# Both layer norms' normalised tiles made on GpSimd instead of ScalarE

## The chip, the cores and the metric

The kernel runs on one core of one Trainium2 chip. Its time is the device time of one execution in microseconds (us). The engines are TensorE (PE in the profile, with PEld for its weight loads), VectorE (DVE), ScalarE (ACT), GpSimd (POOL) and SyncE (SP), which issues most of the DMAs. Each engine runs its own list of instructions in order; they meet through semaphores.

## The reference

The kernel computes one transformer block over x of shape (8, 512, 128), that is 8 batches of 512 tokens with 128 channels. Only what matters here:

```python
def _layernorm(x, axis=-1, eps=1e-05):
    m = jnp.mean(x, axis=axis, keepdims=True)
    v = jnp.var(x, axis=axis, keepdims=True)
    return (x - m) / jnp.sqrt(v + eps)

x = x + attention(_layernorm(x))     # 16 heads of 8 channels, rotary, causal softmax, W_proj
x = x + experts(_layernorm(x))       # gate logits, 8 Sinkhorn rounds, top-64 tokens for each of 8 experts
```

The gate logits and the expert products read the second norm; q, k and v read the first.

## The kernel before, in words

A batch's 512 tokens lie as 4 tiles of 128 tokens by 128 channels (`X[:, TB * b + t, :]`, `TB` = 4). VectorE takes each tile's mean and variance (`statistics`, `statistics2`), into `MV` for the first norm and `MV2` for the second. GpSimd turns them, in the helper `rstd` (L812 to L821), into the inverse root `RSTD` and into `SHIFT` = -mean * inverse root. ScalarE then makes each normalised tile as scale * x + shift, in `normalize_x` (L699, instruction L703, into `XN`) and `normalize_x2` (L707, instruction L711, into `XN2`). TensorE transposes `XN` and `XN2` (L503) and projects the result. The first batch's tiles are made by VectorE (L982). The profile leaves out the numbers of buffers: `XN2`, `MV2`, `RSTD2` and `SHIFT2` stand in it as `XN`, `MV`, `RSTD` and `SHIFT`, and the lines tell them apart; `YS` is an arena that holds the rows of q and k (`QP`, `KZ`) and the exponentials (`PT`).

The eight batches run one after another, each in four stages s = 0 to 3 of four heads. The order is written out by hand: the table `STEP` (L46) lists the steps of a stage, and each engine walks it and issues its own part. The steps that the prediction speaks of are:

- `u` 0 to 9: TensorE forms scores of the next stage (L470), and VectorE takes their row maxima (L928);
- `n`: VectorE writes minus the maxima (L939, L942);
- `mx`: TensorE transposes them (L516) and ScalarE copies them next to q (L686, into `YS`, 8x1024). The first score chunk of the stage waits for that copy;
- `c` 0 to 7 and, in the next stage, `w` 8 and 9: TensorE forms a chunk of transposed scores (L483), ScalarE takes its exponential (L732), and GpSimd zeroes what lies above the diagonal (`causal`, L844), in eight pieces z = 0 to 7 of a stage. The last two pieces follow `w` 8 and `w` 9;
- `v` 0, 3, 1, 2: TensorE multiplies the exponentials of the stage before by the values (L495). `v` 2, the last, waits for all eight pieces; ScalarE then copies the sums (L740).

Other work is tied to a place in this table: (stage, step). In stages 0 and 1 the next batch's q and k are projected, rotated and split into three bfloat16 parts (L828, L832 on GpSimd, L726 on ScalarE, L909 on VectorE). In stages 1 and 2 the batch before gets its projection, its second statistics, `rstd` at (1, `x` 4), its normalised tiles at (2, `w` 9), the transposes at (2, `x` 4) and the logits at (3, `x` 2). After the eighth batch the same is done once more for it, between the first expert products, and the Sinkhorn rounds, the top-64 search and the weighted sum follow (from about 414 us of the span).

Of the kernel before, what the change touches and what calls it, by code (L numbers as in the profile page):

```python
# [9 lines left out]
ACT = mybir.ActivationFunctionType  # L10
ALU = mybir.AluOpType
AX = mybir.AxisListType

B, T, C = 8, 512, 128
H, HD = 16, 8
E = 8
P = 128
TB = T // P
# [41 lines left out]
CUT_V = {(1, "c", 4): (0, 2)}  # L60
PART_ORDER = [(0, 0), (1, 0), (1, 1), (0, 1), (1, 2), (0, 2)]
SUBTRACT = {(1, "u", 2): (1, 0), (1, "u", 3): (0, 0), (1, "c", 1): (0, 1), (1, "u", 6): (1, 1)}
NORMALIZE = (0, "w", 9)

STATISTICS2 = (1, "x", 3)
RSTD2_AT = (1, "x", 4)
NORMALIZE2 = (2, "w", 9)
# [92 lines left out]
def build(nc, x_in, w_qkv, w_swap, w_proj, gate_w, experts, rope, tri, ident, small, out):  # L160
    ctx = ExitStack()
    with ctx:
        def sb(name, shape, dt=F32):
            return ctx.enter_context(nc.sbuf_tensor(name, shape, dt))

        def sem(name):
            return ctx.enter_context(nc.semaphore(name))
# [33 lines left out]
        NHALF = sb("NHALF", [P, B * TB])  # L201
        ONER = sb("ONER", [2, PAIRS // 2, T], BF16)

        X = sb("X", [P, B * TB, C])
# [6 lines left out]
        ST = sb("ST", [P, B * TB, 6])  # L211
        MV = sb("MV", [P, B * TB, 2])
        RSTD = sb("RSTD", [P, B * TB])
        SHIFT = sb("SHIFT", [P, B * TB])
        TC = sb("TC", [P, T])
        TS = sb("TS", [P, T])
        RES = [sb(f"RES{w}", [P, T]) for w in range(2)]
# [11 lines left out]
        ST2 = sb("ST2", [P, TB, 6])  # L229
        MV2 = sb("MV2", [P, TB, 2])  # L230
        RSTD2 = sb("RSTD2", [P, TB])
        SHIFT2 = sb("SHIFT2", [P, TB])
        XN2S = sb("XN2S", [P, T])

        KT = sb("KT", [P, B, TB, E])
# [71 lines left out]
        ln_rstd = sem("ln_rstd")  # L307
        xn_ready = sem("xn_ready")
        ln2_stats = sem("ln2_stats")
        ln2_rstd = sem("ln2_rstd")  # L310
        xn2_ready = sem("xn2_ready")
        resid = [sem("q_residual"), sem("k_residual")]
        part = [sem("q_part"), sem("k_part")]
# [369 lines left out]
        def _(act):  # L683
# [10 lines left out]
            def spread_v(dst, src):  # L694
# [1 line left out]
                    last = act.activation(dst[:, t].rearrange("p (h d) -> p h d", d=2 * VS)[:, :, 0:HD],  # L696
                                          src[:, t].rearrange("p (h d) -> p h d", d=HD), ACT.Copy)
                return last
            def normalize_x(b):  # L699

                for t in range(TB):
                    tile = bass.ds(TB * b + t, 1)
                    last = act.activation(XN[:, t, :], X[:, tile, :].rearrange("p a c -> p (a c)"), ACT.Identity,  # L703
                                          scale=RSTD[:, tile], bias=SHIFT[:, tile])
                last.then_inc(xn_ready, 1)

            def normalize_x2(b):  # L707

                act.wait_ge(ln2_rstd, b + 1)
                for t in range(TB):  # L710
                    last = act.activation(XN2[:, t, :], X[:, bass.ds(TB * b + t, 1), :].rearrange("p a c -> p (a c)"),  # L711
                                          ACT.Identity, scale=RSTD2[:, t:t + 1], bias=SHIFT2[:, t:t + 1])
                last.then_inc(xn2_ready, 1)

            def y_taken(bt): take(bt, "yT", YT[:, :], MB[:, :])
            def xn2_taken(bt):
                if not isinstance(bt.b, int) or bt.b > 1:
# [38 lines left out]
            def one(bt):  # L756
                for s in range(4):
                    vb, vs = (bt.b, s - 1) if s > 0 else (bt.b - 1, 3)
                    for kind, i in STEP:
                        if kind == "c":  # L760
                            exps(bt.b, s, i)
                        elif kind == "w" and (s > 0 or bt.prev):
                            exps(vb, vs, i)
                        elif kind == "mx":
                            max_rows_taken(bt, bt.par, s)
                        elif (kind, i) == ("v", LAST_V) and s % 2 == 0 and (s > 0 or bt.prev):
                            values_taken(vb, vs)
                        elif kind == "x" and bt.extra(s, i) in extras:
                            extras[bt.extra(s, i)](bt)
                        if bt.nxt and (s, kind, i) in CUT:  # L770
                            cut(bt.b + 1, *CUT[s, kind, i])
                        if bt.nxt and (s, kind, i) == NORMALIZE:
                            normalize_x(bt.b + 1)
                        if bt.prev and (s, kind, i) == NORMALIZE2:
                            normalize_x2(bt.b - 1)

            act.wait_ge(ln_rstd, 2)
            batches(act, one)
            end = Batch(B, 0, order=MISC_END)

# [6 lines left out]
            values_taken(B - 1, 3)  # L787
            y_taken(end)
            copy_outputs(0)
            normalize_x2(B - 1)  # L790
            copy_outputs(1)
            xn2_taken(end)

# [13 lines left out]
        @block.gpsimd  # L807
        def _(pool):
            pool.memset(NHALF[:, :], -0.5)
            pool.memset(ONES[:, :], 1.0).then_inc(built, 1)  # L810

            def rstd(n, stats, mv, dst, shift, done):  # L812

                pool.wait_ge(stats, n)
                pool.nop(nofuse=True)
                pool.tensor_scalar(dst, mv[:, :, 1], LN_EPS, None, ALU.add)
                pool.tensor_scalar(shift, mv[:, :, 0], -1.0, None, ALU.mult)
                pool.drain()
                pool.tensor_tensor(dst, dst, NHALF[:, 0:dst.shape[1]], ALU.pow)
                pool.drain()  # L820
                pool.tensor_tensor(shift, shift, dst, ALU.mult).then_inc(done, 1)  # L821

            def rotate(bt, w):
                b = bt.b + 1
                pool.wait_ge(misc_free, bt.misc(("qs", "ks")[w]) + 1)
                if not (isinstance(b, int) and b == 0):
                    pool.wait_ge(part[w], 3 * b)
                pool.tensor_tensor(RES[w][:, :], TC[:, :], TS[:, :], ALU.add).then_inc(resid[w], 1)  # L828

            def subtract(b, w, i):  # L830
                pool.wait_ge(part[w], 3 * b + i + 1)
                pool.tensor_tensor(RES[w][:, :], RES[w][:, :], PARTS[w][:, i, :], ALU.subtract).then_inc(resid[w], 1)  # L832

            def causal(b, s, z):

                c = z + 2 if z >= 2 else 2 * z + 1
                pool.wait_ge(exp_done, 4 * NC * b + NC * s + c + 1)
                pool.nop(nofuse=True)
                if z < 2:
                    v = PT[s % 2][:, c - 1:c + 1, 0:P]  # L840
                else:
                    cols = [col // P for _, _, col in CHUNKS[c]]
                    v = PT[s % 2][:, c, :].rearrange("p (a t) -> p a t", a=TB)[:, 0:TB:cols[1] - cols[0], :]
                pool.affine_select(out=v, in_=v, pattern=[[0, 2], [1, P]], compare_op=ALU.is_ge, fill=0.0,  # L844
                                   base=0, channel_multiplier=-1).then_inc(causal_done, 1)

            rstd(1, ln_stats, MV[:, 0:TB], RSTD[:, 0:TB], SHIFT[:, 0:TB], ln_rstd)
            pool.wait_ge(xn_ready, 1)
            pool.memset(ONER[:, :, :], 1.0).then_inc(built, 1)
            for i in range(2):  # L850
                pool.memset(KZ[i][1][:, :, :].rearrange("p a t -> p (a t)").bitcast(U32), 0).then_inc(built, 1)
            rstd(3, ln_stats, MV[:, TB:], RSTD[:, TB:], SHIFT[:, TB:], ln_rstd)

            def one(bt):
                for s in range(4):
                    for kind, i in STEP:
                        vb, vs = (bt.b, s - 1) if s > 0 else (bt.b - 1, 3)
                        if kind == "c" and (i >= 4 or i % 2 == 1):
                            causal(bt.b, s, i - 2 if i >= 4 else i // 2)
                        if kind == "w" and (s > 0 or bt.prev):  # L860
                            causal(vb, vs, i - 2)
                        if bt.nxt and (s, kind, i) in ROTATE:
                            rotate(bt, ROTATE[s, kind, i])
                        if bt.nxt and (s, kind, i) in SUBTRACT:
                            subtract(bt.b + 1, *SUBTRACT[s, kind, i])
                        if bt.prev and (s, kind, i) == RSTD2_AT:
                            rstd(bt.b, ln2_stats, MV2, RSTD2[:, :], SHIFT2[:, :], ln2_rstd)

            batches(pool, one)
            causal(B - 1, 3, 6)  # L870
            causal(B - 1, 3, 7)
            rstd(B, ln2_stats, MV2, RSTD2[:, :], SHIFT2[:, :], ln2_rstd)


            order = [(b, t) for b in range(DIRECT) for t in OTHERS[b]]
            for j, (b, t) in enumerate(order):
                x = X[:, TB * b + t, :]
                pool.wait_ge(weighted, j + 1)
# [417 lines left out]
```

## Time and profile before

| | before |
|---|---|
| median of 3 runs | 516.52 us (516.19 to 518.79) |
| the profiled execution: its time, its span | 517.8 us, 516.1 us |
| granted TensorE clock, mean | 0.948 |
| busy over the span: PE, DVE, ACT, POOL | 82%, 78%, 61%, 40% |

The span runs from the first to the last instruction, and the profiled execution's own time is 1.7 us longer. Busy times of different engines overlap; an engine's idle time costs something only where another one waits for what it does next.

### The profile page before, as it was taken

The page shows a single profiled execution, that of the slowest core. Times are in us where ns is not written, and L with a number is a line of the kernel's source. Part 1 is how long each engine was busy: PE and PEld are TensorE (multiplying, and loading weights), DVE is VectorE, ACT ScalarE, POOL GpSimd, SP SyncE. Part 2 cuts the span into 40 slices and gives each one's busy share as a digit, 9 for nine tenths or more (in the row PEclk, how much of TensorE's full clock was granted, in tenths as well). Part 3 has the DMA queues.
Part 4 walks back from the last instruction along what each step waited for, and adds up shares of the span by engine and source line. Part 5 has one row for each costly group of instructions (what it writes and reads, how often), then busy time and mean ns, then how long its engine had stood idle before and what let it go on. Part 6 is the DMA issues. An engine that isn't in the chain of part 4 may idle for free.

```text
span 516.1 us, 9496 instructions
## 1 busy us (share of the span) xinstructions
PE 425.1 (82%) x2827; PEld 206.2 (40%) x2827; DVE 402.4 (78%) x1620; ACT 315.7 (61%) x620; POOL 208.4 (40%) x387
## 2 busy tenths in 40 slices
PE   4358889888998889899898989989989677898563
PEld 3133443454444445444344534435543343332221
DVE  6977786787878778877887887788882279997997
ACT  1013675677868668785876878587787413440971
POOL 4140742372366337425643742564344100000795
PEclk9765998999999999999999999999999969999799
DMA  8750360045025203601620360162002010010112
GB/s 256 210 149 1 102 144 3 0 133 134 1 70 140 59 0 124 144 3 49 163 57 1 120 147 3 43 164 60 3 1 63 8 33 20 22 41 0 41 61 81
DMA packets 28432, 36.83 MB, mean 71 GB/s; under 512 B 2144, under 2 KB 24224, under 8 KB 26912
## 3 DMA queue, kind: packets, MB, share of 16 engines
q1 hardware_dynamic: 27312, 34.68, 24.7%
q10 hardware_dynamic: 1072, 1.57, 1.1%
q8 instruction: 22, 0.36, 0.3%
q14 instruction: 26, 0.21, 0.1%
HBM read 19.41 MB, written 16.78 MB: 70 GB/s over the span
## 4 chain that ended last, share of the span: by engine, by line
PE 46%; ACT 19%; DVE 17%; POOL 5%; issue 5%; DMA 3%; POOLq 2%; SPq 1%; DVEq 1%; ACTq 0%
PE PVB L495 10%; ACT YS L732 8%; PE ROWB L470 8%; PE CHB L483 8%; PE MB L527 6%; PE MB L503 3%; POOL RES L832 3%; PE ROWB L621 3%; ACT YS L686 3%; ACT XN L711 2%; DVE YS L1217 2%; ACT PARTS L726 2%; PE CHB L621 2%; PE MB L537 2%; ACT XN L703 2%
## 5 line engine op out<-in xcount | busy, mean ns | idle before, releaser
L928 DVE CUSTOM_DVE_ANT_0 JUNK<-ROWB,TRI 128x384 bf16<-128x384 f32 (+3 forms) x512 | 221.5, 486 | 52.2 <-PE ROWB L470 50.8
L732 ACT ACTIVATE YS<-CHB 128x512 f32<-128x512 f32 x320 | 170.5, 613 | 56.8 <-PE CHB L483 56.6
L844 POOL TENSOR_SCALAR_AFFINE_SELECT YS<-YS 128x256 f32<-128x256 f32 x256 | 104.4, 412 | 174.3 <-ACT YS L732 165.7
L483 PE MATMUL CHB<-YS 104*128 104x384 bf16 (+3 forms) x512 | 116.8, 303 | 19.0 <-ACT YS L686 10.5
L470 PE MATMUL ROWB<-YS 96*128 96x384 bf16 (+3 forms) x512 | 121.2, 309 | 13.7 <-DVE MX L928 5.9
L495 PE MATMUL PVB<-YS,VP 128*32 128x512 f32 (+3 forms) x1024 | 96.4, 446 | 0.2 <-POOL YS L844 0.2
L470 PEld LDWEIGHTS ROWB<-YS 96*128 96x128 bf16 x512 | 44.1, 100 | 87.3 <-issue 39.9
L483 PEld LDWEIGHTS CHB<-YS 104*128 104x128 bf16 x512 | 43.6, 98 | 59.3 <-ACT YS L732 24.3
L686 ACT ACTIVATE YS<-MB 8x1024 bf16<-8x1024 bf16 x32 | 32.5, 1016 | 22.0 <-PE MB L516 21.6
L495 PEld LDWEIGHTS PVB<-YS,VP 128*32 128x32 f32 x1024 | 32.6, 109 | 31.0 <-POOL YS L844 17.4
L621 PE MATMUL CHB<-WEXP,XS 128*128 128x512 f32 x64 | 34.2, 641 | 12.5 <-DVE X L1223 12.5
L928 DVE DVE_READ_ACCUMULATOR2_ANT MX<- 128x1 f32 x512 | 42.4, 83 | 0.0
L879 POOL TENSOR_TENSOR SUM<-YS 128x512 f32<-128x512 f32 x10 | 12.7, 1270 | 71.8 <-ACT YS L803 71.8
L803 ACT ACTIVATE YS<-YS,W 128x128 f32<-128x128 f32 x80 | 24.1, 387 | 21.4 <-DVE W L1191 17.5
L832 POOL TENSOR_TENSOR RES<-RES,PARTS 128x512 f32<-128x512 f32 x28 | 31.9, 1159 | 10.5 <-ACT PARTS L726 10.5
L621 PE MATMUL ROWB<-WEXP,XS 128*128 128x512 f32 x56 | 29.4, 633 | 2.3 <-DVE X L1223 2.3
L726 ACT ACTIVATE PARTS<-RES 128x512 bf16<-128x512 f32 x35 | 22.2, 635 | 2.5 <-POOL RES L832 2.3
L703 ACT ACTIVATE XN<-X,SHIFT,RSTD 128x128 f32<-128x128 f32 x28 | 11.5, 483 | 19.0 <-POOL SHIFT L821 19.0
L711 ACT ACTIVATE XN<-X,SHIFT,RSTD 128x128 f32<-128x128 f32 x32 | 13.2, 483 | 15.4 <-POOL SHIFT L821 15.4
L783 ACT ACTIVATE YS<-ROWB 128x1024 f32<-128x1024 f32 x10 | 10.2, 1021 | 19.4 <-PE ROWB L621 19.4
L621 PEld LDWEIGHTS CHB<-WEXP,XS 128*128 128x128 f32 x64 | 11.5, 202 | 25.0 <-issue 25.0
L828 POOL TENSOR_TENSOR RES<-TC,TS 128x512 f32<-128x512 f32 x14 | 17.8, 1274 | 8.4 <-DVE TS L921 8.4
(132 smaller groups left out, 510.4 us busy)
## 6 DMA issues: line engine op xcount, KB each, us to landing
YS<-parts_scratch SPq DMA_DIRECT2D x28, 384.0 KB, 7.5
parts_scratch<-PARTS SPq DMA_DIRECT2D x15, 384.0 KB, 2.5
parts_scratch<-PARTS SPq DMA_DIRECT2D x15, 256.0 KB, 2.1
X<-in_x SPq DMA_DIRECT2D x8, 256.0 KB, 4.8
xn_scratch<-XN2S SPq DMA_DIRECT2D x8, 256.0 KB, 2.0
XS<-xn_scratch SPq DMA_DIRECT2D x8, 256.0 KB, 2.6
out<-X SPq DMA_DIRECT2D x8, 256.0 KB, 2.3
parts_scratch<-PARTS SPq DMA_DIRECT2D x15, 128.0 KB, 1.8
```

Of the source, the lines that this page charges most:

```text
L470: last = pe.matmul(ROWP[BANK[u]][:, col:col + keys], QP[par][0:ROWS_K, pair, P * qb:keys], KZ[par][i % 2][0:ROWS_K, pair, 0:keys], start=T ...
L483: last = pe.matmul(CH[BANK[c]][:, col:col + n], KZ[par][i % 2][0:ALL_K, pair, P * kb:P * kb + P], QP[par][0:ALL_K, pair, P * kb:T], start= ...
L495: last = pe.matmul(PVB[32 * i:32 * i + 32, P * kb:T], VP[par][:, v:v + 32], PT[s % 2][:, c, col:col + T - P * kb], start=(kb == 0 and s % ...
L527: pe.matmul(MB[:, :], weight, XNT[:, :], start=True, stop=True).then_inc(misc_full, 1)
L621: last = pe.matmul(buffer(n, half), XS[b % 2][:, P * t:P * t + P], WEXP[:, 4 * half:4 * half + 4, :].rearrange("p e o -> p (e o)"), start= ...
L686: act.activation(dst, src, ACT.Copy).then_inc(misc_free, 1)
L726: act.activation(PARTS[w][:, i, :], RES[w][:, :], ACT.Copy).then_inc(part[w], 1)
L732: act.activation(PT[s % 2][:, c, :], CH[BANK[c]], ACT.Exp).then_inc(exp_done, 1)
L803: last = act.activation(WY[j % 2][:, e, :], outputs(TB * b + t, e), ACT.Copy, scale=weight(b, t, e))
L832: pool.tensor_tensor(RES[w][:, :], RES[w][:, :], PARTS[w][:, i, :], ALU.subtract).then_inc(resid[w], 1)
L844: pool.affine_select(out=v, in_=v, pattern=[[0, 2], [1, P]], compare_op=ALU.is_ge, fill=0.0, base=0, channel_multiplier=-1).then_inc(causa ...
L928: last = dve.tensor_tensor_reduce(out=JUNK[BANK[u]][:, col:col + n], in0=ROWP[BANK[u]][:, col:col + n], in1=TRI[:, T - n:T], scale=1.0, sc ...
```

## The change

`SHIFT` and `SHIFT2` go, with the two instructions in `rstd` that made them and one of its drains. GpSimd makes the tiles itself, in one `tensor_scalar` a tile: (x - mean) * inverse root, with the two numbers of each token read from `MV` and `RSTD`. ScalarE's two functions go. The second norm's tiles keep their place (2, `w` 9). The first norm's move from (0, `w` 9) of the batch before to (3, `c` 7) of two batches before, and those of the second batch are made ahead of the loop.

```diff
-NORMALIZE = (0, "w", 9)
+NORMALIZE = (3, "c", 7)
@@ ScalarE
-            def normalize_x(b):
-                for t in range(TB):
-                    tile = bass.ds(TB * b + t, 1)
-                    last = act.activation(XN[:, t, :], X[:, tile, :].rearrange("p a c -> p (a c)"), ACT.Identity,
-                                          scale=RSTD[:, tile], bias=SHIFT[:, tile])
-                last.then_inc(xn_ready, 1)
-            def normalize_x2(b):
-                act.wait_ge(ln2_rstd, b + 1)
-                ...
-            act.wait_ge(ln_rstd, 2)
@@ GpSimd
-            def rstd(n, stats, mv, dst, shift, done):
+            def rstd(n, stats, mv, dst):
                 pool.wait_ge(stats, n)
                 pool.nop(nofuse=True)
                 pool.tensor_scalar(dst, mv[:, :, 1], LN_EPS, None, ALU.add)
-                pool.tensor_scalar(shift, mv[:, :, 0], -1.0, None, ALU.mult)
                 pool.drain()
-                pool.tensor_tensor(dst, dst, NHALF[:, 0:dst.shape[1]], ALU.pow)
-                pool.drain()
-                pool.tensor_tensor(shift, shift, dst, ALU.mult).then_inc(done, 1)
+                return pool.tensor_tensor(dst, dst, NHALF[:, 0:dst.shape[1]], ALU.pow)
+            def normalize_x(b):
+                pool.wait_ge(misc_full, 1 if b == 1 else Batch(b - 2, b % 2, prev=b > 2).misc("xnT") + 1)
+                for t in range(TB):
+                    n = TB * b + t
+                    last = pool.tensor_scalar(XN[:, t, :], X[:, n, :], MV[:, n, 0:1], RSTD[:, n:n + 1],
+                                              ALU.subtract, ALU.mult)
+                last.then_inc(xn_ready, 1)
+            def normalize_x2(b, before):
+                if b > 0:
+                    pool.wait_ge(misc_full, before + 1)
+                for t in range(TB):
+                    last = pool.tensor_scalar(XN2[:, t, :], X[:, TB * b + t, :], MV2[:, t, 0:1], RSTD2[:, t:t + 1],
+                                              ALU.subtract, ALU.mult)
+                last.then_inc(xn2_ready, 1)
@@ GpSimd, in the loop over batches
                         if bt.prev and (s, kind, i) == RSTD2_AT:
+                            rstd(bt.b, ln2_stats, MV2, RSTD2[:, :])
+                            pool.drain()
+                        if bt.prev and (s, kind, i) == NORMALIZE2:
+                            normalize_x2(bt.b - 1, Batch(bt.b - 1, 0).misc("xn2T") if bt.b > 1 else 0)
+                        if bt.b < B - 2 and (s, kind, i) == NORMALIZE:
+                            normalize_x(bt.b + 2)
```

ScalarE's list before, from stage 2 of one batch to stage 0 of the next; `XN2` and `XN` are the two norms' tiles.

```order
L732 ACTIVATE YS<-CHB 128x512 x4
L711 ACTIVATE XN2<-X,SHIFT2,RSTD2 128x128 x4
L686 ACTIVATE YS<-MB 8x1024
L740 ACTIVATE OT<-PVB 128x512
L732 ACTIVATE YS<-CHB 128x512 x8
L686 ACTIVATE XN2S<-MB 128x512
L732 ACTIVATE YS<-CHB 128x512 x2
L686 ACTIVATE YS<-MB 8x1024
L732 ACTIVATE YS<-CHB 128x512 x10
L703 ACTIVATE XN<-X,SHIFT,RSTD 128x128 x4
L686 ACTIVATE YS<-MB 8x1024
```

The same stretch of ScalarE's list now: both groups of four are gone, and the copy of the maxima (8x1024) follows the exponentials directly.

```order
L713 ACTIVATE YS<-CHB 128x512 x4
L683 ACTIVATE YS<-MB 8x1024
L721 ACTIVATE OT<-PVB 128x512
L713 ACTIVATE YS<-CHB 128x512 x8
L683 ACTIVATE XN2S<-MB 128x512
L713 ACTIVATE YS<-CHB 128x512 x2
L683 ACTIVATE YS<-MB 8x1024
L713 ACTIVATE YS<-CHB 128x512 x10
L683 ACTIVATE YS<-MB 8x1024
```

GpSimd's list before, from the end of stage 1 of one batch to the first rotation of the next one; the 21 pieces are z6 and z7 of stage 1, all 16 of stages 2 and 3 and three of the next stage 0.

```order
L844 AFFINE_SELECT YS<-YS 128x2x128 x5
L816 TENSOR_SCALAR RSTD2<-MV2 128x4
L817 TENSOR_SCALAR SHIFT2<-MV2 128x4
L819 TENSOR_TENSOR RSTD2<-RSTD2,NHALF 128x4
L821 TENSOR_TENSOR SHIFT2<-SHIFT2,RSTD2 128x4
L844 AFFINE_SELECT YS<-YS 128x2x128 x21
L828 TENSOR_TENSOR RES0<-TC,TS 128x512
```

GpSimd's list now: the second norm's tiles stand behind the first two of the 21 pieces, and the first norm's tiles between the last piece that follows a `c` step of stage 3 and the two that follow `w` 8 and `w` 9 of the next stage 0.

```order
L834 AFFINE_SELECT YS<-YS 128x2x128 x5
L791 TENSOR_SCALAR RSTD2<-MV2 128x4
L793 TENSOR_TENSOR RSTD2<-RSTD2,NHALF 128x4
L834 AFFINE_SELECT YS<-YS 128x2x128 x2
L809 TENSOR_SCALAR XN2<-X,MV2,RSTD2 128x128 x4
L834 AFFINE_SELECT YS<-YS 128x2x128 x14
L800 TENSOR_SCALAR XN<-X,MV,RSTD 128x128 x4
L834 AFFINE_SELECT YS<-YS 128x2x128 x5
L818 TENSOR_TENSOR RES0<-TC,TS 128x512
```

The lists of TensorE, VectorE and SyncE are unchanged.

## Rows read from the trace of the kernel before

**Rows 1.** Windows: one batch. Window: length, busy (instructions) by engine, clock, DMA
```profile
224.30:269.60 45.30, 40.91 (x326) 20.41 (x324) 36.39 (x158) 34.19 (x67) 21.72 (x42) 1.00 0.29 77
```

**Rows 2.** Waits of the whole span. Who <- for whom: us in total, times, longest
```profile
ACT XN L711 <- POOL SHIFT L821: 15.4, 8, 4.3
...
PE CHB L483 <- ACT YS L686: 10.5, 14, 1.0
```

**Rows 3.** Chain of waits, start of a stage 2. Start, length, what
```profile
208.36 1.47 ACT XN L711 x4
...
210.04 1.02 ACT YS L686
```

**Rows 4.** Timeline, POOL, the same place. Start, length, what [idle before]
```profile
206.24 0.24 POOL L816 TENSOR_SCALAR RSTD<-MV 128x4 f32<-128x4 f32 x1
206.54 0.23 POOL L817 TENSOR_SCALAR SHIFT<-MV 128x4 f32<-128x4 f32 x1
...
208.13 0.20 POOL L821 TENSOR_TENSOR SHIFT<-SHIFT,RSTD 128x4 f32<-128x4 f32 x1
208.28 0.78 POOL L844 TENSOR_SCALAR_AFFINE_SELECT YS<-YS 128x256 f32<-128x256 f32 x2
```

**Rows 5.** Timeline, PE and its weight loads, the same place
```profile
209.10 0.16 PEld L495 LDWEIGHTS PVB<-YS,VP 128*32 128x32 f32 x8 [0.67 <-POOL YS L844]
...
209.68 0.39 PE L470 MATMUL ROWB<-YS 96*128 96x384 bf16 x2
211.11 0.39 PE L483 MATMUL CHB<-YS 104*128 104x512 bf16 x1 [1.04 <-ACT YS L686]
```

**Rows 6.** Chain of waits, start of the next batch's stage 0
```profile
226.86 1.53 ACT XN L703 x4
...
228.42 1.02 ACT YS L686
```

**Rows 7.** Timeline, PE, the same place
```profile
228.67 0.39 PE L470 MATMUL ROWB<-YS 96*128 96x384 bf16 x2
229.49 0.39 PE L483 MATMUL CHB<-YS 104*128 104x512 bf16 x1 [0.43 <-ACT YS L686]
```

**Rows 8.** Timeline, POOL, the same place
```profile
225.84 0.43 POOL L844 TENSOR_SCALAR_AFFINE_SELECT YS<-YS 128x256 f32<-128x256 f32 x1
...
226.99 0.41 POOL L844 TENSOR_SCALAR_AFFINE_SELECT YS<-YS 128x256 f32<-128x256 f32 x1 [0.72 <-ACT YS L732]
```

**Rows 9.** Timeline, DVE, the same place
```profile
225.83 0.18 DVE L942 SCALAR_TENSOR_TENSOR NMX<-MX,NMX 128x16 bf16<-128x16 f32 x1
...
229.21 0.56 DVE L928 CUSTOM_DVE_ANT_0 JUNK<-ROWB,TRI 128x384 bf16<-128x384 f32 x1 [0.52 <-PE ROWB L470]
```

**Rows 10.** Lines by shape, POOL. Busy us, mean ns of one, idle before
```profile
L844 POOL TENSOR_SCALAR_AFFINE_SELECT YS<-YS 128x256 f32<-128x256 f32 x256 | 104.4, 412 | 174.3 <-ACT YS L732 165.7
...
L883 POOL TENSOR_TENSOR SUM<-SUM 128x128 f32<-128x128 f32 x10 | 4.6, 456 | 0.8
...
L816 POOL TENSOR_SCALAR RSTD<-MV 128x4 f32<-128x4 f32 x9 | 2.1, 238 | 14.1 <-DVE MV L901 13.5
...
L816 POOL TENSOR_SCALAR RSTD<-MV 128x28 f32<-128x28 f32 x1 | 0.3, 296 | 16.3 <-DVE MV L901 16.3
```

**Rows 11.** Timeline after the last batch
```profile
408.62 1.65 ACT L711 ACTIVATE XN<-X,SHIFT,RSTD 128x128 f32<-128x128 f32 x4 [4.33 <-POOL SHIFT L821]
...
410.41 0.63 PE L503 MATMUL MB<-IDF,XN 128*128 128x128 f32 x4 [2.76 <-ACT XN L711]
```

**Rows 12.** Instructions of a line, DVE. Duration ns min/median/max, first and last start
```profile
L909 DVE CAST PARTS<-RES x7: 1361/1364/1367, 63.7 to 338.4; 128x512 bf16<-128x512 f32 x7
...
L1011 DVE CAST PARTS<-RES x6: 415/426/426, 18.1 to 24.9; 128x512 bf16<-128x512 f32 x6
```

**Rows 13.** Timeline, POOL and PE, where the second norm's tiles are next needed
```profile
212.78 0.41 POOL L844 TENSOR_SCALAR_AFFINE_SELECT YS<-YS 128x256 f32<-128x256 f32 x1 [3.73 <-ACT YS L732]
...
215.05 0.66 PE L503 MATMUL MB<-IDF,XN 128*128 128x128 f32 x4
```

More of the change, by code:

```diff
@@ L213, in build @@
         RSTD = sb("RSTD", [P, B * TB])
-        SHIFT = sb("SHIFT", [P, B * TB])
         TC = sb("TC", [P, T])
@@ L231, in build @@
         RSTD2 = sb("RSTD2", [P, TB])
-        SHIFT2 = sb("SHIFT2", [P, TB])
         XN2S = sb("XN2S", [P, T])
@@ L309, in build @@
         ln2_stats = sem("ln2_stats")
-        ln2_rstd = sem("ln2_rstd")
         xn2_ready = sem("xn2_ready")
@@ L698, in spread_v @@
                 return last
-            def normalize_x(b):
-                for t in range(TB):
-                    tile = bass.ds(TB * b + t, 1)
-                    last = act.activation(XN[:, t, :], X[:, tile, :].rearrange("p a c -> p (a c)"), ACT.Identity,
-                                          scale=RSTD[:, tile], bias=SHIFT[:, tile])
-                last.then_inc(xn_ready, 1)
-            def normalize_x2(b):
-                act.wait_ge(ln2_rstd, b + 1)
[L710 to L713, printed above, removed]
             def y_taken(bt): take(bt, "yT", YT[:, :], MB[:, :])
@@ L771, in one @@
                             cut(bt.b + 1, *CUT[s, kind, i])
[L772 to L775, printed above, removed]
-            act.wait_ge(ln_rstd, 2)
             batches(act, one)
@@ L789, in _ @@
             copy_outputs(0)
-            normalize_x2(B - 1)
             copy_outputs(1)
@@ L845, in causal @@
                                    base=0, channel_multiplier=-1).then_inc(causal_done, 1)
-            rstd(1, ln_stats, MV[:, 0:TB], RSTD[:, 0:TB], SHIFT[:, 0:TB], ln_rstd)
+            rstd(1, ln_stats, MV[:, 0:TB], RSTD[:, 0:TB]).then_inc(ln_rstd, 1)
             pool.wait_ge(xn_ready, 1)
@@ L851, in _ @@
                 pool.memset(KZ[i][1][:, :, :].rearrange("p a t -> p (a t)").bitcast(U32), 0).then_inc(built, 1)
-            rstd(3, ln_stats, MV[:, TB:], RSTD[:, TB:], SHIFT[:, TB:], ln_rstd)
+            rstd(3, ln_stats, MV[:, TB:], RSTD[:, TB:])
+            pool.drain()
+            normalize_x(1)
             def one(bt):
@@ L866, in one @@
                         if bt.prev and (s, kind, i) == RSTD2_AT:
-                            rstd(bt.b, ln2_stats, MV2, RSTD2[:, :], SHIFT2[:, :], ln2_rstd)
+                            rstd(bt.b, ln2_stats, MV2, RSTD2[:, :])
+                            pool.drain()
+                        if bt.prev and (s, kind, i) == NORMALIZE2:
+                            normalize_x2(bt.b - 1, Batch(bt.b - 1, 0).misc("xn2T") if bt.b > 1 else 0)
+                        if bt.b < B - 2 and (s, kind, i) == NORMALIZE:
+                            normalize_x(bt.b + 2)
             batches(pool, one)
@@ L871, in _ @@
             causal(B - 1, 3, 7)
-            rstd(B, ln2_stats, MV2, RSTD2[:, :], SHIFT2[:, :], ln2_rstd)
+            rstd(B, ln2_stats, MV2, RSTD2[:, :])
+            pool.drain()
+            normalize_x2(B - 1, Batch(B - 1, 1, nxt=False).misc("xn2T"))
             order = [(b, t) for b in range(DIRECT) for t in OTHERS[b]]
```

## Prediction

> **What bounds the kernel now.** I read the windows of one batch first. A batch takes 45.3 us, in which TensorE is busy for 40.9, VectorE for 36.4, ScalarE for 34.2 and GpSimd for 21.7 [rows 1]. No engine is full. TensorE is the fullest, with about 4.4 us idle a batch, and GpSimd could take 8 more tiles a batch by its share alone. So the question is which of TensorE's idle time ends on the normalised tiles. The list of waits names it: the first score chunk of a stage waits for ScalarE's copy of the maxima 14 times, 10.5 us in all and at most 1.0 each [rows 2]. ScalarE itself sits idle 15.4 us in 8 places until `SHIFT` is there [rows 2].
>
> The chain of waits at the start of a stage 2 shows why: it runs through the four tiles of the second norm and then through the copy, which begins at 210.04 and takes 1.02 [rows 3]. TensorE finished the step before (`u` 4) at 209.68 + 0.39 = 210.07 and starts its chunk only at 211.11, idle for 1.04 [rows 5]. At the start of the next stage 0 the chain has the same form with the first norm's tiles [rows 6], but TensorE's idle is only 0.43 [rows 7]. Seven places of the first kind (batches 1 to 7) and six of the second (1 to 6) make 7 x 1.04 + 6 x 0.43 = 9.9 of the 10.5. This is all that taking the tiles off ScalarE can give back inside the batches.
>
> **The second norm's tiles, batches 1 to 7.** Removed from ScalarE's list are 4 tiles (1.65 us as seen after the last batch [rows 11]) and the wait ahead of them. The copy can then start when TensorE's transposes are in, which is before 208.6 (the values product follows them, and its last part begins at 209.10 [rows 5]). It ends by about 209.6, ahead of 210.07. The chunk then starts at 210.07, 1.04 earlier. What binds next is TensorE's own work and VectorE's last row maxima ahead of `u` 4, so I count no more than this. 7 x 1.04 = 7.3 us gained.
>
> On GpSimd, `rstd` becomes shorter: 206.54 - 206.24 = 0.30 for one `SHIFT` instruction and 208.28 - 208.13 = 0.15 for the other [rows 4]. So pieces z6 and z7 come 0.45 earlier, about 207.83 to 208.61, which removes most of TensorE's 0.67 wait for them [rows 5]. That is worth nothing further, as `u` 4 follows VectorE. The four new tiles stand behind z7. They run from 208.6 to 208.6 + 4d, where d is the cost of one tile on GpSimd. The transposes that need them come at 215.05, and the next piece of the mask at 212.78 [rows 13], each 1.0 earlier with the rest. The mask is delayed from d = (211.7 - 208.6)/4 = 0.78 on, and it gates only the values product of the next stage. So the new work here lies in GpSimd's own wait of 3.73 us and costs nothing.
>
> **The first norm's tiles, batches 1 to 6.** They leave ScalarE at stage 0 and go to GpSimd at the end of stage 3, in six batches (b = 0 to 5 make them for b + 2; those for batch 1 run ahead of the loop beside the first score rows and cost nothing). GpSimd has no spare time there: z6 started at 225.84, right behind z5, and z7 ended at 226.99 + 0.41 = 227.40 [rows 8]. In the new order both stand behind four tiles. The two pieces back to back take 0.78 [rows 4], so z7 ends at 225.84 + 4d + 0.78 = 226.62 + 4d. Behind it waits the last values product on TensorE, and behind that `u` 4 and the chunk. That product takes 209.68 - 209.10 = 0.58 [rows 5], so here it ran from 228.67 - 0.58 = 228.09 [rows 7]. With 0.04 from the end of z7 to it (209.06 to 209.10 [rows 4, 5]), it is late by 226.66 + 4d - 228.09 = 4d - 1.43. The 0.43 that ScalarE's tiles cost there [rows 7] comes off. The net cost at each of the six places is 4d - 1.86, and never below -0.43.
>
> **What d is.** The trace has no GpSimd operation with a number per partition. From below, 256 columns with one input take 412 ns, so 128 columns without any fixed part would take 206. Two inputs of 128x128 take 456. The existing `TENSOR_SCALAR` takes 238 ns for 4 columns and 296 for 28, 2.4 ns a column more, which at 128 columns gives 296 + 100 x 2.4 = 538. From above, if the two arithmetic steps were passes of their own, 2 x 456 = 912 [rows 10]. I take 0.50 us, between the nearest shape (0.456) and the nearest operation (0.538). So each place costs 4 x 0.50 - 1.86 = 0.14, and six cost 0.9 us.
>
> The Trainium skill, in GPSIMD Engine Reference, section Engine selection, says that GpSimd is about half VectorE's speed with two inputs but nearly at line rate with one. The rows agree in part: the one-input select takes 412 ns for twice the columns that two inputs do in 456 [rows 10]. By that rule alone the tile would be near the cheap end, and the forecast would be that of the second rival below.
>
> **After the last batch.** The second norm's tiles stand alone in the path to the logits. ScalarE starts them at 408.62, and TensorE transposes at 410.41, 1.79 later [rows 11]. GpSimd starts them 0.45 earlier by the shorter `rstd`, plus about 0.05 for a wait between engines that is gone, and takes 4d: at d = 0.50 it is 4 x 0.50 - 1.79 - 0.50 = -0.3. I take -0.2, since ScalarE's tiles overlap a little. In general the term is 4(d - 0.50) - 0.2.
>
> **The sum.** -7.3 + 0.9 - 0.2 = -6.6 us. The profiled execution took 517.8 (span 516.1 and 1.7 around it), so it would take 511.2. The median of the runs is 516.52, 1.3 lower, so I predict 509.9. With d left open, the sum is 6(4d - 1.86) + 4(d - 0.50) - 0.2 - 7.3 = 28d - 20.7, which is zero at d = 0.74.
>
> **Rivals.**
>
> *The tile is dear on GpSimd, and TensorE waits for the mask* (slower or no gain). Place: the last values product of stage 0, six times. It takes most of the gain from d = 0.64 on and all of it from d = 0.74, and at d = 0.91 gives 28 x 0.91 - 20.7 = +4.8, so 521.3. For it: no row shows such an operation, and it has two arithmetic steps and two numbers to fetch for each partition. Against it: all plain operations in rows 10 are under 0.55 at 128 columns. Chance 0.18.
>
> *The tile is cheap.* At d under 0.36 each of the six places reaches its floor of -0.43: -7.3 - 2.6 - 0.2 - 4 x 0.14 = -10.7, so 505.9. For it: the select's rate [rows 10]. Against it: the 2.4 ns a column of the same operation. Chance 0.22.
>
> *GpSimd's reads hold VectorE up.* A cast of 128x512 takes 1.364 us while GpSimd subtracts and 0.426 alone [rows 12], so VectorE's instructions can stand until a GpSimd one ends. At the start of stage 0 the second minus-maximum instruction reads two tensors (225.83, 0.18 us [rows 9]), and would meet the first new tile. The most that it could wait is one tile, 0.50, six times: 3.0, so 512.9. Against it: VectorE then has 0.52 idle at 229.21 [rows 9], which would swallow it, and its row maxima keep their durations while GpSimd works. Chance 0.12.
>
> The Trainium skill, in SBUF — State Buffer, section Who interferes with whom, states this as a rule: a port pair is shared, taken whole for one instruction, and a VectorE instruction with two SBUF inputs or in a two-port mode blocks against a reading GpSimd one. The slow cast agrees with it. By that rule the minus-maximum is blocked for up to a tile, which is the rival's price.
>
> *The gain is given back.* The chunk starts a microsecond earlier, but the stage ends on ScalarE's exponentials or on VectorE's maxima, and nothing is left: 516. For it: VectorE and ScalarE are busy 36.4 and 34.2 of 45.3 [rows 1]. Against it: at that place both wait for TensorE, which waits for the copy. Chance 0.10.
>
> **How the numbers follow.** The forecast has d from 0.36 to 0.64 and the full gain of 7.3: 28d - 20.7 from -10.6 to -2.8, so 505.9 to 513.7, with chance 0.38. The measurement tells about 0.5% (2.6 us) from no change. Faster by more than that are the forecast (0.38), the cheap tile (0.22) and most of the held-up VectorE (0.10): 0.70. Within it are the gain given back (0.10), the rest of VectorE's (0.02) and the dear tile between 0.64 and 0.83 (0.04): 0.16. Slower is the rest of the dear tile: 0.14. For the range I go from 505.0, just under the cheap tile, to 517.5, which leaves out the dear tile beyond break-even and little else.
>
> **What would show it.** In the profile of the changed kernel, TensorE's wait for the maxima copy falls from 10.5 us to under 3. ScalarE's busy time falls by 60 tiles, and its idle before `SHIFT` is gone. The new tile's mean says d, and TensorE's wait for L834's pieces is where d's price stands: about 0.6 us at each stage 0. VectorE's second minus-maximum instruction stays at 0.18 if GpSimd does not hold it. A batch becomes about 0.9 us shorter: 45.3 to 44.4. I am wrong if d is above 0.74, if the chunk of stage 2 still waits for something else at the same time as now, or if the batch keeps its length though d is small.

## The result, and the profile after

The changed kernel is slower. Its median is 524.71 us (524.14 to 528.99, 4 runs) against 516.56 (516.19 to 518.79, 4 runs), a ratio of 1.0167 with a 95% interval of 1.0105 to 1.0228. The forecast was 509.9, so it had the wrong sign, and the time lies above the range. In the profiled executions the spans are 522.5 and 516.1 us.

The window of one batch has the columns of [rows 1]: ScalarE's busy time fell from 34.2 to 31.1 us, GpSimd's rose from 21.7 to 27.5, and the batch grew by one microsecond.

```profile
227.22:273.54 46.32, 40.62 (x325) 20.39 (x324) 36.26 (x158) 31.11 (x58) 27.46 (x49) 1.00 0.29 75
```

The list of waits answers to [rows 2]. TensorE's wait for the copy of the maxima, 10.5 us before, has gone to 0.6.

```profile
PE ROWB L467 <- issue: 11.5, 7, 2.7
...
PE PVB L492 <- POOL YS L834: 8.4, 7, 1.4
...
PE CHB L480 <- ACT YS L683: 0.6, 1, 0.6
```

Two waits have come in its place. The values products wait 8.4 us for the mask, and the score rows 11.5 us for something that the profile does not name. The same two rows of the kernel before are small:

```profile
PE ROWB L470 <- issue: 4.3, 3, 2.2
...
PE PVB L495 <- POOL YS L844: 0.2, 1, 0.2
```

At the start of a stage 2 the order came out as predicted. GpSimd's timeline answers to [rows 4], here from a later batch: the two `SHIFT` instructions are gone, and the tiles follow z7.

```profile
299.95 0.23 POOL L791 TENSOR_SCALAR RSTD<-MV 128x4 f32<-128x4 f32 x1
300.33 1.05 POOL L793 TENSOR_TENSOR RSTD<-RSTD,NHALF 128x4 f32<-128x4 f32 x1
301.58 0.78 POOL L834 TENSOR_SCALAR_AFFINE_SELECT YS<-YS 128x256 f32<-128x256 f32 x2 [0.20 <-issue]
302.34 3.15 POOL L809 TENSOR_SCALAR XN<-X,MV,RSTD 128x128 f32<-128x128 f32 x4
```

TensorE's timeline answers to [rows 5], in the batch before that one: `u` 4 is followed by the chunk without a gap, where 1.04 us was lost.

```profile
257.00 0.39 PE L467 MATMUL ROWB<-YS 96*128 96x384 bf16 x2
257.22 0.38 PE L480 MATMUL CHB<-YS 104*128 104x512 bf16 x1
```

At the start of the next stage 0, GpSimd and TensorE answer to [rows 7, 8]. The four tiles hold z6 and z7 back for 3.1 us. The weight load of the last values product stands idle for 2.05 before it, but that overlaps other matmuls: what TensorE itself loses is 1.35. The list's 8.4 us are six such places, 1.35 to 1.37 each, and one of 0.22 late in the span, which the kernel before has too.

```profile
273.52 3.13 POOL L800 TENSOR_SCALAR XN<-X,MV,RSTD 128x128 f32<-128x128 f32 x4
276.61 0.77 POOL L834 TENSOR_SCALAR_AFFINE_SELECT YS<-YS 128x256 f32<-128x256 f32 x2
```

```profile
277.43 0.16 PEld L492 LDWEIGHTS PVB<-YS,VP 128*32 128x32 f32 x8 [2.05 <-POOL YS L834]
277.43 0.64 PE L492 MATMUL PVB<-YS,VP 128*32 128x256 f32 x8 [1.35 <-POOL YS L834]
```

The lines by shape answer to [rows 10]. A tile costs 0.80 us, not 0.50.

```profile
L809 POOL TENSOR_SCALAR XN<-X,MV,RSTD 128x128 f32<-128x128 f32 x32 | 25.2, 798 | 0.2 <-issue 0.2
L800 POOL TENSOR_SCALAR XN<-X,MV,RSTD 128x128 f32<-128x128 f32 x28 | 21.9, 796 | 0.2 <-issue 0.2
```

After the last batch, the timeline answers to [rows 11]. From the start of the tiles to the transposes it takes 3.3 us instead of 1.8.

```profile
413.43 3.15 POOL L809 TENSOR_SCALAR XN<-X,MV,RSTD 128x128 f32<-128x128 f32 x4 [0.17 <-issue]
416.72 0.63 PE L500 MATMUL MB<-IDF,XN 128*128 128x128 f32 x4 [3.78 <-POOL XN L809]
```

By the waits alone, these pieces come close to the difference of the two spans, 522.5 - 516.1 = 6.4 us: the unnamed wait 11.5 - 4.3 = 7.2, the mask 8.4 - 0.2 = 8.2, the copy 0.6 - 10.5 = -9.9 and the end 1.0 (the transposes are 6.3 later than before, the attention's sum at L960 5.3 later) give 6.5. This count is not a chain, and two terms of about 1.6 us that it leaves out cancel in it: a lower clock after some waits (below) costs that much more than before, and stage 2 gains more than the wait that is gone (shown with the lengths of a batch, behind the experiments).

**What the unnamed wait is.** It stands at one place, `u` 0 of stage 3, the first score rows of the next batch. These rows need that batch's q and k, which SyncE loads from DRAM (four loads of 384 KB, each about 7 us from issue to landing). First the kernel before, then the changed one: the issue of the loads, and TensorE's score rows.

```profile
252.05 1.73 SPq L368 DMA_DIRECT2D YS<-parts_scratch  x4
```

```profile
262.16 0.39 PE L470 MATMUL ROWB<-YS 96*128 96x512 bf16 x1
```

```profile
254.41 1.72 SPq L365 DMA_DIRECT2D YS<-parts_scratch  x4
...
264.63 0.38 PE L467 MATMUL ROWB<-YS 96*128 96x512 bf16 x1 [1.30 <-issue]
```

Before, the rows ran 10.11 us after the issue and did not wait. Now they run 10.22 after it and do. All seven batches of the kernel before have this distance, 9.7 to 10.3 us, the three that waited and the four that did not; so the four had no time to spare either. The issue hangs on stage 1 and did not move with stage 2. So before the change the loads landed just in time, and whatever stage 2 gained was bound to be lost at this wait. This was a reading until the loads were cut in the experiments below.

Two of the seven waits cost more than their length. After the one of 2.19 at 309.46 the granted clock fell to its lower level for some four microseconds (windows, columns as in [rows 1]; 0.56 and 0.59 are mostly 1.2 GHz in place of 2.4). The same followed the wait of 2.69 that ended at 170.60, and in the kernel before the one of 2.23 that ended at 78.43: the second fence has that place.

```profile
310.00:312.00 2.00, 0.35 (x3) 0.25 (x4) 0.00 (x0) 0.00 (x0) 0.00 (x0) 1.00 0.28 102
312.00:314.00 2.00, 2.00 (x14) 0.47 (x11) 1.83 (x5) 0.60 (x1) 0.41 (x1) 0.56 0.00 0
314.00:316.00 2.00, 2.00 (x21) 1.23 (x20) 0.79 (x4) 1.02 (x1) 0.00 (x0) 0.59 0.00 0
```

```profile
80.00:82.00 2.00, 2.00 (x20) 1.17 (x20) 1.48 (x6) 1.02 (x1) 0.19 (x1) 0.57 0.00 0
82.00:84.00 2.00, 2.00 (x12) 0.71 (x8) 0.68 (x3) 0.36 (x1) 0.00 (x0) 0.58 0.00 0
```

From these score rows to the first ones of the next stage it takes 10.38 and 10.28 us with the lower clock and 8.76 without it (8.75 in the kernel before), and in the shorter first batch 9.68 and 8.11. So each such stretch costs about 1.6 us, and the changed kernel has one more of them than the kernel before.

### The profile page after: what moved, and what is told of

Same layout as the page of the kernel before. It is cut to its first block, busy times and chain, and to the rows that moved or that the text cites. A ratio compares the mean times of both kernels' runs of the same rounds, so it can differ in the third digit from the quotient of the medians.

```text
span 522.5 us, 9475 instructions
## 1 busy us (share of the span) xinstructions
PE 423.7 (81%) x2827; PEld 205.9 (39%) x2827; DVE 401.7 (77%) x1620; ACT 292.5 (56%) x560; POOL 250.7 (48%) x427
## 4 chain that ended last, share of the span: by engine, by line
PE 47%; DVE 23%; POOL 12%; issue 9%; ACT 5%; DVEq 2%; DMA 2%; POOLq 0%; ACTq 0%
PE PVB L492 11%; PE ROWB L467 9%; PE CHB L480 6%; PE MB L524 6%; DVE JUNK L927 5%; POOL RES L822 4%; POOL YS L834 3%; POOL XN L800 3%; PE MB L500 3%; PE ROWB L618 3%; ACT YS L713 3%; DVE YS L1216 2%; PE CHB L618 2%; PE MB L534 2%; DVE CHB L1216 2%
## 5 line engine op out<-in xcount | busy, mean ns | idle before, releaser
L467 PE MATMUL ROWB<-YS 96*128 96x384 bf16 (+3 forms) x512 | 122.7, 313 | 20.5 <-issue 11.5
L492 PE MATMUL PVB<-YS,VP 128*32 128x512 f32 (+3 forms) x1024 | 97.5, 451 | 8.4 <-POOL YS L834 8.4
L878 POOL TENSOR_TENSOR SUM<-YS 128x512 f32<-128x512 f32 x10 | 12.7, 1275 | 70.2 <-ACT YS L778 70.2
L822 POOL TENSOR_TENSOR RES<-RES,PARTS 128x512 f32<-128x512 f32 x28 | 31.9, 1160 | 10.5 <-ACT PARTS L707 10.5
L809 POOL TENSOR_SCALAR XN<-X,MV,RSTD 128x128 f32<-128x128 f32 x32 | 25.2, 798 | 0.2 <-issue 0.2
L800 POOL TENSOR_SCALAR XN<-X,MV,RSTD 128x128 f32<-128x128 f32 x28 | 21.9, 796 | 0.2 <-issue 0.2
L618 PEld LDWEIGHTS CHB<-WEXP,XS 128*128 128x128 f32 x64 | 11.5, 203 | 24.9 <-issue 24.9
```

The costliest lines, as they stand in the source:

```text
L467: last = pe.matmul(ROWP[BANK[u]][:, col:col + keys], QP[par][0:ROWS_K, pair, P * qb:keys], KZ[par][i % 2][0:ROWS_K, pair, 0:keys], start=T ...
L492: last = pe.matmul(PVB[32 * i:32 * i + 32, P * kb:T], VP[par][:, v:v + 32], PT[s % 2][:, c, col:col + T - P * kb], start=(kb == 0 and s % ...
L618: last = pe.matmul(buffer(n, half), XS[b % 2][:, P * t:P * t + P], WEXP[:, 4 * half:4 * half + 4, :].rearrange("p e o -> p (e o)"), start= ...
L800: last = pool.tensor_scalar(XN[:, t, :], X[:, n, :], MV[:, n, 0:1], RSTD[:, n:n + 1], ALU.subtract, ALU.mult)
L809: last = pool.tensor_scalar(XN2[:, t, :], X[:, TB * b + t, :], MV2[:, t, 0:1], RSTD2[:, t:t + 1], ALU.subtract, ALU.mult)
```

## The experiments

Each median is set against the kernel before in the same session: 516.54 in the first, 518.24 in the second, 517.1 in the third. Where two kernels of different sessions are compared, the sessions' own difference stands in the result, so I give what the medians say and what the ratios say.

**One norm at a time.** In the first, the first norm's tiles go back to ScalarE at (0, `w` 9):

```diff
-NORMALIZE = (3, "c", 7)
+NORMALIZE = (0, "w", 9)
@@ ScalarE: normalize_x as before the change; GpSimd: SHIFT made again, its normalize_x gone
```

> Only the second norm's tiles on GpSimd (at (2, w 9)); the first norm's stay on ScalarE at (0, w 9) with SHIFT. Theory A: the loss has three parts, (1) z6 and z7 behind the first norm's tiles at stage 0, (2) the gain at stage 2 is taken back in batches 1 to 6 because TensorE then waits before the next batch's first score rows for the loads of its q and k rows, which do not come earlier, (3) the tail. Here (1) is absent, (2) leaves only batch 7's gain of about 1.3, and the tail costs 1.0: about the time of the kernel before, 515.5 to 518, with TensorE idle 1 to 2.7 us before those score rows in each batch. Theory B: the gain of stage 2 is real and kept, and the first norm's tiles cost more than their wait shows: 508 to 511. Theory C: GpSimd's reads slow VectorE wherever the tiles run: 519 or more, with longer VectorE instructions.

Measured: 518.83 (516.68 to 524.0, 10 runs), ratio 1.0049 (1.0012 to 1.0086). The profiled execution has a span of 515.2. The stage 2 gain does not show in the time, against theory B. The unnamed wait stands in all seven batches (1.50, 1.72, 2.30, 1.23, 1.14, 1.14 and 0.79 us), and the mask's is gone. The median is 0.8 over theory A's range, and the runs scatter by 7 us.

In the second, the other half:

```diff
@@ ScalarE: normalize_x2 as before the change; GpSimd: SHIFT2 made again, its normalize_x2 gone
```

> Only the first norm's tiles on GpSimd (at (3, c 7)); the second norm's stay on ScalarE with SHIFT2. Theory A: 0.96 us a batch in six batches for z7, less half a microsecond at the start, no long waits before the next batch's score rows, no cost in the tail: 521 to 522.5. Theory B: the first norm's tiles carry the whole loss of 8 us plus the 7 that the second norm's give: 529 to 532. Theory C: somewhere between, with VectorE's minus-maximum instruction near 0.8 instead of 0.18.

Measured: 522.98 (520.57 to 523.88, 7 runs), ratio 1.0103 (1.0067 to 1.0139), half a microsecond over theory A's range. TensorE waits for the mask as long as in the changed kernel, and for the score rows as little as before:

```profile
PE PVB L494 <- POOL YS L857: 8.4, 7, 1.4
...
PE ROWB L469 <- issue: 4.5, 3, 2.7
```

VectorE's second minus-maximum instruction, the one that theory C was about, has a mean of 193 ns here and in the changed kernel, against 182 before, far from 0.8 us. Theory C falls.

**The first norm's tiles where GpSimd is idle.**

```diff
-NORMALIZE = (3, "c", 7)
+NORMALIZE = (3, "w", 9)
```

> The changed kernel with NORMALIZE = (3, w 9): the first norm's tiles stand behind z7 of stage 2, where GpSimd waits over 3 us, not ahead of z6 of stage 3. Theory A: the wait for z7 at stage 0 goes and ScalarE's 0.43 there is saved, six times, but the next batch's q and k rows bound the batch less the later they are read, so most of it shows: 1.4 us a batch off the changed kernel's 524.7, so 515 to 517. Theory B: what counts is that GpSimd has 3.2 us more work in each half of a batch, wherever it stands: within 2 us of the changed kernel.

Measured: 514.33 (512.44 to 517.25, 10 runs), ratio 0.9948 (0.9915 to 0.9981). The same work on the same engine, moved 7 us earlier within stage 3 (1.8 us behind its first score rows in place of 8.9), is 10 to 11 us faster than the changed kernel and 2 faster than the one before, 0.7 under theory A's range. The tiles now run from 216.51 to 219.64, in a gap, and z7 comes in time. The unnamed wait stays (10.7 us in 7 places), as theory A says.

**What a tile's price is made of.** 40 instructions (the expectation says 42) on GpSimd after its last `rstd`, in eight groups:

```diff
             rstd(B, ln2_stats, MV2, RSTD2[:, :], SHIFT2[:, :], ln2_rstd)
+            m, r = MV[:, 0, 0:1], RSTD[:, 0:1]
+            pool.drain()
+            for n in range(6):
+                pool.tensor_scalar(SCR[:, 128 * n:128 * n + 128], TS[:, 0:128], m, r, ALU.subtract, ALU.mult)
+            ...
```

> The kernel before with 42 further GpSimd instructions after its last rstd, where GpSimd has nothing to do for some 70 us: tensor_scalar on 128 columns with two numbers per partition, on 64 and on 512 columns, with two constants, with one number, with one constant (128 and 512), and a copy. If the price of a tile is by the column (5 to 6 ns each at two steps), 64 columns take about 0.5 and 512 about 2.7 to 3 us, and one step costs clearly less than two. If it is the fetch of the two numbers, 64 columns take about 0.65, 512 about 1.6, and two constants about 0.45. The kernel's own time should change by under 3 us.

Measured, in lines by shape (L878, L881, L884: two numbers per partition, two steps; L887: two constants; L890: one number; L893, L896: one constant; L899: a copy):

```profile
L878 POOL TENSOR_SCALAR SCR<-TS,MV,RSTD 128x128 f32<-128x128 f32 x6 | 4.7, 793 | 0.2 <-issue 0.2
L884 POOL TENSOR_SCALAR SCR<-TS,MV,RSTD 128x512 f32<-128x512 f32 x2 | 4.2, 2122 | 0.2 <-issue 0.2
L890 POOL TENSOR_SCALAR SCR<-TS,MV 128x128 f32<-128x128 f32 x6 | 3.9, 659 | 0.2 <-issue 0.2
L887 POOL TENSOR_SCALAR SCR<-TS 128x128 f32<-128x128 f32 x6 | 3.8, 658 | 0.2 <-issue 0.2
L881 POOL TENSOR_SCALAR SCR<-TS,MV,RSTD 128x64 f32<-128x64 f32 x6 | 3.7, 637 | 0.2 <-issue 0.2
L893 POOL TENSOR_SCALAR SCR<-TS 128x128 f32<-128x128 f32 x6 | 3.1, 537 | 0.2 <-issue 0.2
L896 POOL TENSOR_SCALAR SCR<-TS 128x512 f32<-128x512 f32 x2 | 2.9, 1488 | 0.2 <-issue 0.2
L899 POOL COPY SCR<-TS 128x128 f32<-128x128 f32 x6 | 1.6, 320 | 0.1
```

At 128 columns one step with a constant takes 537 ns. A second step adds 121, and numbers per partition in place of constants add 122 for one and 135 for two. From 128 to 512 columns the two-step form adds 3.5 ns a column and the one-step form 2.5. So neither expectation held alone. By the slope from 128 to 512 columns some 350 ns of the 793 do not depend on the columns (793 less 128 x 3.5), and the rest does; the step from 64 to 128 columns is only 2.4 ns a column (793 less 637), so this split is an estimate and the price is not a straight line. The one run of this kernel took 517.06 us, so the extra work cost nothing there.

**The loads cut in two.** In each kernel below, the next batch's q and k come in two lots:

```diff
-                    load_rows(sp, bt.b + 1, 1 - bt.par, 0)
-                    load_rows(sp, bt.b + 1, 1 - bt.par, 1)
+                    for w in range(2):
+                        sp.wait_ge(stored[w], 48 * bt.b + 96)
+                        load_rows(sp, 1 - bt.par, w, 0, 2)
+                    for w in range(2):
+                        load_rows(sp, 1 - bt.par, w, 2, PAIRS)
@@ TensorE, before the score rows
+                if u == 0 and s < 2:
+                    for w in range(2):
+                        pe.wait_ge((first_loaded, loaded)[s][w], 32 * b + 32)
```

> The kernel before, with the loads of the next batch's q and k rows cut in two: first those of pairs 0 and 1, which the first score rows read, then the other six pairs, which nothing reads before the next stage. The bytes are the same. Theory A (the wait ahead of the next batch's first score rows, 4.3 us in three places here, is for these loads): the three waits go, and the stretch at half clock behind the longest, so 510.5 to 513.5. Theory B (the wait is for instructions or something else that a cut load doesn't change): 516 to 518, with the waits as they were.

> The changed kernel with the same cut of the loads. Theory A: the seven waits of 11.5 us in all go, with some 2 us of half clock; what stays against the cut kernel before is the first norm's tiles ahead of z6 (6 x 1.0 to 1.4) and the tail (1.0), less the stage 2 gain that is now kept (7 x 1.0 to 1.3): so 510 to 514, level with the cut kernel before within 2 us, where the uncut ones are 8 apart. Theory B: 523 to 526, 8 above the cut kernel before.

Measured: 512.57 (512.22 to 512.67, ratio 0.9889, 0.9854 to 0.9924) for the kernel before, and 510.31 (509.65 to 510.56, ratio 0.9844, 0.9809 to 0.9880) for the changed one. The wait before the score rows is gone from both traces, so it was for the loads. The changed kernel gets 14 us (medians) to 17 us (ratios) faster by the cut and the one before 4 to 6, and with it the change is 2 us faster instead of 8 slower. The waits and the lower clock behind them account for this: 11.5 + 2 x 1.6 = 14.7 in the changed kernel, 4.3 + 1.6 = 5.9 in the one before.

> Only the second norm's tiles on GpSimd, and the loads cut in two. With uncut loads this kernel was 2 us slower than the one before, and I hold that its gain at stage 2 was only hidden by the wait for the loads. Against the cut kernel before (512.6): 1.4 us a batch from the halves of a batch in the traces (26.7 to 25.3), seven times, less 1.0 for the tail, so 503 to 505. If stage 2's gain ends elsewhere too (VectorE, the exponentials), it stays at 512 to 514.

Measured: 504.07 (503.39 to 504.78), ratio 0.9756 (0.9736 to 0.9776). Uncut, this kernel was no faster than the one before; cut, it is 8.5 us faster than the cut one before by the medians and 6.9 by the ratios. The hidden gain is there.

**Shorter tiles at the bad place.** This kernel leaves out the second half of the columns (`W` = 64) of the first norm's tiles of batches 1 to 7.

```diff
-                    last = pool.tensor_scalar(XN[:, t, :], X[:, n, :], MV[:, n, 0:1], RSTD[:, n:n + 1],
+                    last = pool.tensor_scalar(XN[:, t, 0:W], X[:, n, 0:W], MV[:, n, 0:1], RSTD[:, n:n + 1],
```

> The changed kernel with cut loads, in which GpSimd makes only the first 64 of the 128 columns of the first norm's tiles of batches 1 to 7 (the other half of XN is left out, so q, k and v are wrong). A tile of 64 columns takes 0.637 instead of 0.793. If the price at stage 0 is 4 tiles' length less the slack, as the formula 4d - 1.86 has it, four tiles are 0.64 shorter, six times: 3.8 less than the 510.3 of the full tiles, 506 to 507. If the wait for z7 has another cause than the tiles' length (a wait, the switch between operations): 509.5 to 510.5.

Measured: 504.53 (504.24 to 505.3), ratio 0.9762 (0.9743 to 0.9781). That is 5.8 less than with full tiles by the medians and 4.2 by the ratios, where 3.8 was expected; the median lies 1.5 under the range. Here a half tile took 583 ns and four took 2.26 us against 3.13, so 0.87 a batch and 5.2 in six. TensorE's wait for the mask fell from 8.4 to 3.1 us, by 5.3, and the spans differ by the same 5.3 (508.2 and 502.9). The price is the tiles' length, as the formula has it; only my length for the half tile was too long.

**A better version.** The first norm's tiles at (3, `w` 9), the loads cut, and the last batch's four tiles on VectorE, which waits at that point:

```diff
@@ VectorE, after the last statistics2
+            dve.wait_ge(ln_rstd, 2)
+            for t in range(TB):
+                last = dve.tensor_scalar(XN2[:, t, :], X[:, TB * (B - 1) + t, :], MV2[:, t, 0:1], RSTD2[:, t:t + 1],
+                                         ALU.subtract, ALU.mult)
+            last.then_inc(xn2_ready, 1)
```

> The candidate for a better version: the changed kernel with the first norm's tiles at (3, w 9), the loads cut in two, and the last batch's four second-norm tiles on VectorE, which waits there. Theory A: from the 514.3 of the kernel with (3, w 9) alone, less 10.7 for the waits ahead of the score rows, 2 for the half clock and 2 for the tail: 499 to 503. Theory B: 511 to 513, the tail's gain alone.

> The changed kernel with (3, w 9) and the last batch's four second-norm tiles on VectorE, loads uncut. All theories: VectorE made such tiles in 1.12 for four at the start, GpSimd takes 3.15, so the tail is 2.0 shorter than with (3, w 9) alone: 512 to 512.6. If the tail is longer bound by the expert products, nothing comes of it: 514.

Measured: 498.29 (497.94 to 498.96), ratio 0.9619 (0.9584 to 0.9654) with the cut loads, and 512.97 (511.25 to 515.53), ratio 0.9907 (0.9877 to 0.9937), without them. The first is 0.7 under theory A's range, the second 0.4 over its own, and 1.4 to 2.1 us faster than with (3, `w` 9) alone where 2.0 was expected. The four tiles take VectorE 1.12 us:

```profile
389.31 1.12 DVE L1064 TENSOR_SCALAR XN<-X,MV,RSTD 128x128 f32<-128x128 f32 x4 [1.70 <-POOL RSTD L791]
```

The first is the fastest kernel of this study, 3.8% under the one before.

**The length of a batch without the load's wait.** ScalarE copies the values products' sums at the same step of every batch, so two such copies give the batch's length. The cut kernel before, then the cut kernel with the second norm alone on GpSimd, the cut changed kernel, and the last one:

```profile
205.78 0.60 ACT L738 ACTIVATE OT<-PVB 128x512 f32<-128x512 f32 x1
...
250.89 0.60 ACT L738 ACTIVATE OT<-PVB 128x512 f32<-128x512 f32 x1
```

```profile
200.36 0.60 ACT L728 ACTIVATE OT<-PVB 128x512 f32<-128x512 f32 x1
...
244.19 0.60 ACT L728 ACTIVATE OT<-PVB 128x512 f32<-128x512 f32 x1
```

```profile
204.14 0.60 ACT L719 ACTIVATE OT<-PVB 128x512 f32<-128x512 f32 x1
...
248.90 0.60 ACT L719 ACTIVATE OT<-PVB 128x512 f32<-128x512 f32 x1
```

```profile
198.92 0.60 ACT L719 ACTIVATE OT<-PVB 128x512 f32<-128x512 f32 x1
...
242.12 0.60 ACT L719 ACTIVATE OT<-PVB 128x512 f32<-128x512 f32 x1
```

They are 45.11, 43.83, 44.76 and 43.20 us. So the second norm's tiles on GpSimd gain 1.28 a batch, the first norm's at (3, `c` 7) cost 0.93, and the same at (3, `w` 9) gain 0.63. These lengths give the whole account of the changed kernel: -7 x 1.28 + 6 x 0.93 = -3.4 us in the batches, 7.2 more of waits for the loads, 1.6 more of lower clock and 1.0 at the end make 6.4, and the spans differ by 6.4. With the loads cut, -3.4 + 1.0 = -2.4, and those spans differ by -2.6 (508.2 against 510.8). Why stage 2 gains 1.28 where TensorE's wait was 1.04 was not followed up.

## Why the prediction was wrong

*The places and the mechanism at stage 2* were right. The copy's wait went from 10.5 to 0.6 us (under 3 was predicted), and a batch gains 1.28 where 1.04 was forecast, once the loads are out of the way.

*"So I count no more than this. 7 x 1.04 = 7.3 us gained"* is the first step that failed. The sentence names what binds next, TensorE's work and VectorE's maxima, and leaves out the DMA queue. The next batch's rows landed at the very moment when they were read, and the list of waits had three places where the score rows already waited, 4.3 us in all, without a name. I had put them down to nothing. The rival "the gain is given back" stood there with a chance of 0.10, but with ScalarE and VectorE as the takers. The cut loads show that it was this: the waits cost 7.2 us more than before, and the clock 1.6 more, together 8.8 of the 9.0 that stage 2 gained (7 x 1.28). That the 7.2 is also the forecast gain of 7.3 is chance: batch by batch the waits grew by -0.3 to 2.2.

*"I take 0.50 us"* is the term that was mis-sized. The tile takes 0.797. The extrapolation to 538 ns for one step with a constant was exact (537), but that was the wrong operation: the second step and the numbers per partition add 256 ns. The trace bounded d by 0.912, and I chose by the middle of the two nearest rows, both of them cheaper forms. By the formula, 28 x 0.797 - 20.7 = +1.6 us: this error alone takes the forecast from 6.6 us gained to 1.6 lost, the first rival's side. The loads make the rest, and more: +1.6, 7.2 of waits and 1.6 of clock, less 1.7 that stage 2 gained beyond the forecast and 2.4 by which the price at stage 0 stayed under the formula, give 6.3, where the spans differ by 6.4. The medians differ by 8.15 because the profiled execution of the kernel before was 1.3 above its median, and that of the changed kernel 0.45 under.

*The price 4d - 1.86 at each stage 0* held in form, and its slack was too small. At d = 0.797 it gives 1.33. TensorE's wait for the mask is 1.36, where 4d - 1.43 gives 1.76; less the 0.43 of the copy that is 0.93, as the batches show, and the half tiles moved it by their length.

*The end* held: 4(d - 0.50) - 0.2 gives 1.0, and 1.0 was measured.

*GpSimd's reads holding VectorE up* did not happen with the new tiles. By the trace the minus-maximum instruction starts 0.07 to 0.08 us after the first tile in all six places, as the rival wanted, and takes 0.20 to 0.21 us there against 0.18 elsewhere; the tile's row is `273.52 3.13 POOL L800` above.

```profile
273.60 0.21 DVE L941 SCALAR_TENSOR_TENSOR NMX<-MX,NMX 128x16 bf16<-128x16 f32 x1
```

Held for a whole tile it would have taken 0.7 or more. By the Trainium skill's rule in SBUF — State Buffer, section Who interferes with whom, it should have been, if the tile was reading by then. Once the trace looks as the rule has it: at 145.99 the same instruction starts 0.08 after a piece of the mask (145.91, 0.41 long), takes 0.36 and ends with it. GpSimd's recorded starts are rough, so why the tile does not hold it and the piece does stays open. The Trainium skill's rule in GPSIMD Engine Reference, section Engine selection, that one-input work is nearly at line rate, is not borne out for `tensor_scalar`: the same four tiles took GpSimd 3.13 us and VectorE 1.12. With one input tensor GpSimd needs 2.5 ns a column with one step and 3.5 with two, where the one-input mask took 412 ns for 256 columns in all [rows 10].

## What to carry to other kernels

A wait that an engine loses is worth its length only if what the work runs into next is not itself just in time, and DMAs count among these: for each place that comes earlier, look at when the loads read behind it were issued and landed. A wait that the profile gives no name is a wait all the same, and three of them before the change were the warning. On an engine with gaps, the place of moved work decides more than its engine: the same four tiles cost 0.93 us a batch ahead of two urgent instructions and gained 0.63 when they stood most of a stage (7 us) earlier, in a gap.

## What was not expected of the hardware

GpSimd's `tensor_scalar` has a price for each step and for numbers read per partition (537, 658, 659 and 793 ns at 128 columns), while a copy takes 320 and an addition of two tensors of that size 456. A stall of 2.2 us in which all compute engines stood still was followed by some 4 us at mostly 1.2 GHz, which made the values products behind it take 3.3 us (312.91 to 316.21) where the same ones took 2.1 in the kernel before (308.36 to 310.43). The wait's length does not decide this alone. The traces of the seven kernels with uncut loads have ten waits for the score rows of 2.19 us or more. After nine of them the clock fell in this way, and after the longest, 3.10 us in the kernel with (3, `w` 9), it stayed full; it also stayed full after every shorter one, up to 2.04.
